# A fused Swin block on one core: values weighed a tile later in one group, channel sums over 128 columns, late products spread over the prologue

## The chip, the cores and the metric

The kernel runs on 1 core of one Trainium2 chip. The metric is the device time of one execution in microseconds; the figure for the kernel before is the median of 3 runs. The engines are TensorE (PE; its weight loads are PEld), VectorE (DVE), ScalarE (ACT), GpSimd (POOL) and SyncE (SP), which here only starts transfers. Each engine works through its own instruction list in order and waits on semaphores for the others.

## The reference

The input x is 16 images of 64 channels and 16 x 16 pixels, fp32. One Swin transformer block, cut to what matters:

```python
xn = roll(layernorm_over_channels(x) * g1 + b1, (-4, -4))
windows = 8x8 windows of xn                      # 64 windows of 64 tokens, 64 channels
q, k, v = split(windows @ in_w.T + in_b)         # 8 heads of 8
attn = softmax(q @ k.T / sqrt(8)) @ v            # per window and head
y = x + roll_back((attn @ out_w.T + out_b) @ proj_w.T + proj_b)
z = layernorm_over_channels(y) * g2 + b2
result = y + (gelu(z @ fc1_w.T + fc1_b) @ fc2_w.T + fc2_b)   # 64 -> 256 -> 64
```

## The kernel before

**Tiles.** The work is cut into 8 tiles (`TILES`) of 256 token columns. A tile holds two images: image w = 0 on the channel partitions 0 to 63, w = 1 on 64 to 127. Everything is fp32; a product on TensorE shows as two records in the trace (two passes). A transposition of 128 x 128 is one record.

**Stages of a tile k.** VectorE takes statistics (`ln1_stats`), GpSimd makes `rstd` and scales; TensorE transposes (`x_transpose`) and projects q, k and v (`project_qkv`), three tiles ahead (`AHEAD`). ScalarE copies q, k, v out of PSUM; SyncE spreads q and k over four head slots by 8 transfers per tile (`mask_heads`, L238). TensorE forms the scores once with queries on partitions, into `ps_s`, for the row maximum on VectorE (`find_max`, L594), and once transposed, into `ps_t` (`scores_both` interleaves the two, L302). The maximum is transposed on VectorE (`transpose_max`) and spread by GpSimd (`spread_max`, L937), and TensorE subtracts it from the transposed scores (`shift_scores`, L359). ScalarE exponentiates (L825) into `probs`. `weigh_values` (L376) multiplies by values and ones, so sums and weighted values come out together in `ps_u`, image by image. On VectorE `normalise` then does four things in a row: transposition of `ps_u` into `sums` (L608), reciprocal (L610), scaling into `attn_tok` (L614), transposition into `attn` (L621). TensorE's `project_out` (L392) applies output and projection weights, folded into one matrix at the start; VectorE's `residual` (L628) adds x. For the second norm ScalarE squares y, TensorE's `y_sum` (L404) sums y and its square over the 64 channels of each image, ScalarE and VectorE make the variance (`ln2_var`, L642), GpSimd the reciprocal root and its widening (`ln2_rstd`, `ln2_widen`), TensorE spreads it (`y_spread`, L419), VectorE scales (`ln2_scale`, L647).

**The order.** It is written out by hand, engine by engine, in functions named `slot(t)`, called for t = 0 to 7 (TensorE has `first_slot` for t = 0). TensorE's slot t holds, in this order, the first scores group of tile t + 1 with the transposed scores of tile t, the shift of (t, 0), `project_qkv(t + 3)`, values of (t - 1, image 1), `y_sum(t - 2)`, the second scores group, the shift of (t, 1), `x_transpose`, `y_spread`, values of (t, image 0), `project_out(t - 1)`. VectorE's slot t holds `find_max(t + 1, 0)`, statistics, the whole of `normalise(t - 1)`, `ln2_var(t - 2)`, `find_max(t + 1, 1)`, `transpose_max(t + 1)`, `residual(t - 1)`, `ln2_scale(t - 3)`.

**Start and end.** Before slot 1, TensorE makes products of the late weights (`late_products`, `fc1_mean`, `bias_of_v`) and runs products of zeros (`warm_up`, L257). After the slots come four steps of 512 columns of the two-layer net, `fc1` (L433), gelu on ScalarE (L853), `fc2` (L449) and VectorE's `finish` (L708), with what is left of the last tiles between them.

**PSUM.** There are 8 banks: `ps_s` 2, `ps_t` 2, `ps_m` 2, `ps_u`, `ps_o`. `ps_u` holds the weighed values of both images of one tile; it is free when `sums` has been transposed. `ps_o` takes `project_out`, `y_sum` and the late products in turn.

## Time and profile before

| | |
|---|---|
| three runs | 97.44, 100.54, 97.42 us; median 97.44 |
| profiled execution, its own time | 97.66 us |
| its span, first to last instruction | 95.8 us |
| mean granted TensorE clock | 0.997 of full |
| busy: PE, DVE, ACT, POOL | 90%, 67%, 50%, 45% of the span |
| transfers | 5.87 MB, 61 GB/s over the span |

The span starts and ends with an instruction; the execution's own time has 1.86 us more around it. A slice or a busy share is an average over stages with different limits, so each stage has to be read by itself: which engine waits last, and for whom.

### The profile page before, as it was taken

Reading aid. Unit: us, or ns where it says so; the run is one execution under the profiler, and the core shown is the slowest. Engines: PE = TensorE matmul, PEld = TensorE weight load, DVE = VectorE, ACT = ScalarE, POOL = GpSimd, SP = SyncE. Lnnn points to the kernel's source line nnn. Section 1 sums busy time; section 2 is a strip of 40 time slices with the busy share of each in tenths; the row PEclk is TensorE's granted clock in tenths of the full one; section 3 lists DMA queues with packets and bytes.
Section 4 is the critical chain, followed back from the end, with each engine's and each line's share of the span. In section 5 each row is a group of like instructions: output and inputs, shape, how many; then the busy total and the mean of one; then the engine's idle time right before and its main releaser. Section 6 shows DMA issues by size and latency. Waiting matters only on the chain.

```text
span 95.8 us, 4276 instructions
## 1 busy us (share of the span) xinstructions
PE 86.4 (90%) x1810; PEld 55.0 (57%) x1810; DVE 63.8 (67%) x183; ACT 48.1 (50%) x78; POOL 43.5 (45%) x56
## 2 busy tenths in 40 slices
PE   5999999999999699999999889989899967799960
PEld 5987756776755557747666567566665224233330
DVE  5966879818899978957959889798342943403070
ACT  0594815735556447556655443335449654073700
POOL 7988734485056436750740834708343063500000
PEclk9999999999999999999999999999999999999998
DMA  2899110111110111111110101000000000020323
GB/s 36 236 383 403 64 42 14 57 48 42 41 46 29 61 42 56 36 47 42 34 61 28 61 28 41 0 7 0 7 0 7 0 0 7 0 109 0 113 107 112
DMA packets 3747, 5.87 MB, mean 61 GB/s; under 512 B 1136, under 2 KB 1904, under 8 KB 3600
## 3 DMA queue, kind: packets, MB, share of 16 engines
q1 hardware_dynamic: 2864, 3.22, 9.9%
q10 hardware_dynamic: 864, 2.38, 6.6%
q8 instruction: 14, 0.23, 1.1%
q14 instruction: 5, 0.04, 0.2%
HBM read 2.64 MB, written 1.05 MB: 39 GB/s over the span
## 4 chain that ended last, share of the span: by engine, by line
PE 32%; issue 24%; POOL 19%; DVE 15%; DMA 3%; SPq 2%; POOLq 1%; ACT 1%; DVEq 0%
POOL max_x L937 7%; POOL rstd L946 7%; PE ps_t L257 6%; DVE row_max L594 6%; POOL rstd_x L953 5%; DMA masked<-qk 3%; PE ps_t L359 3%; PE ps_u L449 3%; PE ps_m L277 3%; DVE sums L608 2%; PE ps_s L302 2%; PE ps_t L433 2%; PE ps_o L449 2%; PE ps_u L376 2%; SPq L238 2%
## 5 line engine op out<-in xcount | busy, mean ns | idle before, releaser
L825 ACT ACTIVATE probs<-ps_t 128x1024 f32<-128x1024 f32 x16 | 16.4, 1024 | 17.4 <-PE ps_t L359 17.4
L594 DVE TENSOR_REDUCE row_max<-ps_s 128x16 f32<-128x1024 f32 x15 | 18.2, 1216 | 5.2 <-PE ps_s L302 5.2
L302 PE MATMUL ps_t<-masked,qk 32*64 32x256 f32 x272 | 18.7, 387 | 0.4 <-ACT probs L825 0.3
L946 POOL TENSOR_TENSOR rstd<-y_var,minus_half 128x4 f32<-128x4 f32 x8 | 8.3, 1034 | 22.0 <-DVE y_var L642 21.8
L302 PE MATMUL ps_s<-masked,qk 32*64 32x256 f32 x240 | 16.5, 386 | 1.7 <-ACT probs L825 0.7
L359 PE MATMUL ps_t<-max_x,minus_sel 128*128 128x512 f32 x32 | 11.7, 446 | 0.8 <-POOL max_x L937 0.8
L302 PEld LDWEIGHTS ps_s<-masked,qk 32*64 32x64 f32 x240 | 8.3, 131 | 4.3 <-issue 2.8
L376 PE MATMUL ps_u<-probs,vz 128*32 128x64 f32 x512 | 10.5, 222 | 0.0
L376 PEld LDWEIGHTS ps_u<-probs,vz 128*32 128x32 f32 x512 | 7.9, 109 | 3.8 <-issue 2.8
L302 PEld LDWEIGHTS ps_t<-masked,qk 32*64 32x64 f32 x272 | 8.7, 131 | 1.5 <-issue 0.4
L257 PE MATMUL ps_t<-zeros 128*128 128x128 f32 x40 | 8.2, 366 | 1.0 <-DVE zeros L737 1.0
L359 PEld LDWEIGHTS ps_t<-max_x,minus_sel 128*128 128x128 f32 x32 | 4.8, 188 | 6.9 <-POOL max_x L937 3.5
L608 DVE STREAM_TRANSPOSE sums<-ps_u 128x512 f32<-128x512 f32 x8 | 5.7, 712 | 4.5 <-PE ps_u L376 4.4
L922 POOL TENSOR_TENSOR rstd<-var,minus_half 128x4 f32<-128x4 f32 x8 | 8.2, 1025 | 0.7
L257 PEld LDWEIGHTS ps_t<-zeros 128*128 128x128 f32 x40 | 7.1, 265 | 1.7 <-DVE zeros L737 1.0
L937 POOL TENSOR_TENSOR max_x<-max_t,early 128x512 fp32r<-128x512 f32 x6 | 6.3, 1050 | 3.0 <-DVE max_t L602 3.0
L953 POOL TENSOR_SCALAR rstd_x<-rstd 128x256 f32<-128x256 f32 x8 | 6.9, 857 | 0.3
L628 DVE SCALAR_TENSOR_TENSOR y_all<-ps_o,b_out,x_ch 128x256 f32<-128x256 f32 x8 | 3.8, 470 | 4.4 <-PE ps_o L392 4.4
L794 ACT ACTIVATE qk<-ps_m,b_qk 128x512 f32<-128x512 f32 x7 | 4.8, 685 | 3.4 <-PE ps_m L289 3.3
L831 ACT ACTIVATE y_sq<-y_all 128x256 f32<-128x256 f32 x8 | 3.3, 416 | 6.2 <-DVE y_all L628 6.2
L919 POOL TENSOR_SCALAR var<-mv 128x4 f32<-128x4 f32 x8 | 1.6, 197 | 10.4 <-DVE mv L587 10.1
L972 POOL MEMSET masked<- 128x2048 f32 x3 | 5.4, 1806 | 2.0 <-DVE row_max L594 2.0
(102 smaller groups left out, 147.8 us busy)
## 6 DMA issues: line engine op xcount, KB each, us to landing
masked<-qk SPq DMA_DIRECT2D x58, 32.0 KB, 1.9
x_ch<-x_ch_d ACTq DMA_DIRECT2D x1, 1024.0 KB, 8.5
out_d<-result SPq DMA_DIRECT2D x3, 256.0 KB, 2.5
x_tok<-x_tok_d ACTq DMA_DIRECT2D x1, 512.0 KB, 6.5
late<-late_d ACTq DMA_DIRECT2D x1, 352.0 KB, 5.1
x_tok<-x_tok_d SPq DMA_DIRECT2D x2, 128.0 KB, 3.2
x_tok<-x_tok_d ACTq DMA_DIRECT2D x1, 256.0 KB, 4.5
out_d<-result SPq DMA_DIRECT2D x2, 128.0 KB, 2.3
```

The costliest lines, as they stand in the source:

```text
L257: nc.tensor.matmul(ps[:, 0, 0:P], zeros[:], zeros[:], start=True, stop=True)
L302: return nc.tensor.matmul(ps[L * u:L * u + L, g, n * TOK:(n + 1) * TOK], qk[r:r + RG, b, w, t], masked[r:r + RG, b, :, w, t], start=(n == ...
L359: ins = nc.tensor.matmul(ps_t[:, g, :], minus_sel[:, 2 * w + g].rearrange("q u j -> q (u j)"), max_x[:, k % 2, :], start=False, stop=True, ...
L376: ins = nc.tensor.matmul(u5[32 * h:32 * h + 32, w, n, :, g, :], vz[:, k % VB, w, n, SLOTS * g + h, :], probs[:, w, c:c + L], start=True, s ...
L594: nc.vector.tensor_reduce(row_max[:, 16 * w:16 * w + 16], score_bank(k, w)[:].rearrange("q g (h j) -> q (g h) j", j=L), axis=AX.X, op=ALU. ...
L608: nc.vector.transpose(sums[:].rearrange("q n r -> q (n r)"), ps_u[:, 0, :]).then_inc(sums_transposed, 1)
L825: nc.scalar.activation(probs[:, w, :], ps_t[:].rearrange("q g c -> q (g c)"), ACT.Exp).then_inc(probs_done, 1)
L922: nc.gpsimd.tensor_tensor(rstd1[:, b, :], var1[:, b, :], minus_half[:], op=ALU.pow).then_inc(x_rstd_done, 1)
L937: nc.gpsimd.tensor_tensor(max_x[:, k % 2, :].rearrange("q (n i) -> q n i", n=16), max_t[:].unsqueeze(1).to_broadcast([P, 16, 32]), spread1 ...
L946: nc.gpsimd.tensor_tensor(rstd2[:].rearrange("q n w -> q (n w)"), y_var[:].rearrange("q n w -> q (n w)"), minus_half[:], op=ALU.pow).then_ ...
L953: nc.gpsimd.tensor_scalar(rstd2_x[:, k % 2].rearrange("q n (w c) -> q n w c", w=2), rstd2[:].unsqueeze(3).to_broadcast([P, BLK, 2, C]), 1. ...
L972: nc.gpsimd.memset(masked[:, b].rearrange("q h w t -> q (h w t)"), 0.0).then_inc(masked_zeroed[b], 1)
```

## The change

It has five parts.

1. `weigh_values` of both images of tile t - 1 now stand together in slot t, followed by `project_out(t - 2)` (before: `project_out(t - 1)` at the slot's end). `probs` has four buffers in place of two, so exponentiate waits for the values of two tiles back.
2. `y_sum` takes 128 columns as stationary operand: 4 products of 128 x 2 in place of 16 of 32 x 2. It stands at the end of the slot, after `y_spread`.
3. VectorE's `normalise` is split in four. Transposition of the sums and reciprocal stay ahead of `find_max(t + 1, 1)`, with `residual(t - 2)` between the two; scaling and transposition of the attention come behind `transpose_max`. `ln2_var` and `ln2_scale` move to the front of the next slot. ScalarE's squaring of y and GpSimd's `ln2_rstd` and `ln2_widen` move accordingly.
4. The late products are split: those of the output weights between the projections of q, k and of v of tile 0, the bias products between `x_transpose(2)` and `project_qkv(2)`, `fc1_mean` and `bias_of_v` into slot 1. Nine of twelve `warm_up` products behind the first projection go.
5. The end has another order, since the last tiles are one stage further back; the second-to-last spread uses `ps_o`.

The core of the diff:

```diff
-        probs = sb("probs", [P, 2, 1024])
+        probs = sb("probs", [P, 4, 1024])
...
-                        for j in range(4):
-                            c = n * P + 32 * j
-                            src = y_sq[:, c:c + 32] if s else y_all[:, k * TOK + c:k * TOK + c + 32]
-                            ins = nc.tensor.matmul(ps_o[32 * j:32 * j + 32, 0, 4 * n + 2 * s:4 * n + 2 * s + 2], src, ones2,
-                                                   start=True, stop=True, tile_position=(0, 32 * j))
+                        c = n * P
+                        src = y_sq[:, c:c + P] if s else y_all[:, k * TOK + c:k * TOK + c + P]
+                        ins = nc.tensor.matmul(ps_o[:, 0, 4 * n + 2 * s:4 * n + 2 * s + 2], src, ones2,
+                                               start=True, stop=True)
...
                 x_transpose(2)
-                warm_up(2, ps_u)
+                late_products_bias()
                 project_qkv(2)
-                late_products()
-                warm_up(2, ps_u)
                 scores_both(1, 0, 0, 1)
                 shift_scores(0, 1)
                 x_transpose(3)
-                weigh_values(0, 0)
                 scores(1, 1)
                 project_qkv(3)
-                fc1_mean()
-                bias_of_v()
...
                 if t == 1:
+                    fc1_mean()
+                    bias_of_v()
+                    weigh_values(0, 0)
                     weigh_values(0, 1)
                 if tile_ok(t + AHEAD):
                     project_qkv(t + AHEAD)
                 if t >= 2:
+                    weigh_values(t - 1, 0)
                     weigh_values(t - 1, 1)
-                    y_sum(t - 2)
+                    project_out(t - 2)
...
                 if t >= AHEAD:
                     y_spread(t - AHEAD)
-                weigh_values(t, 0)
...
-                project_out(t - 1)
...
+                if t >= 2:
+                    y_sum(t - 2)
...
             project_qk(0)
-            warm_up(4)
+            late_products_out()
+            warm_up(2)
             project_v(0)
-            warm_up(2)
             scores(0, 0)
...
-            warm_up(2, ps_u)
+            warm_up(1, ps_u)
...
+            fc1(0, 0)
+            weigh_values(TILES - 1, 0)
+            weigh_values(TILES - 1, 1)
+            project_out(TILES - 2)
             fc1(0, 1)
+            y_spread(TILES - 3)
             y_sum(TILES - 2)
             fc1(1, 0)
             project_out(TILES - 1)
             fc1(1, 1)
-            y_spread(TILES - 2)
             y_sum(TILES - 1)
             fc2(0)
+            y_spread(TILES - 2)
+            fc1(2, 0)
             y_spread(TILES - 1)
-            fc1(2, 0)
...
-                if k >= 1:
-                    act.wait_ge(values_weighed, 2 * (k - 1) + w + 1)
+                if k >= 2:
+                    act.wait_ge(values_weighed, 2 * (k - 2) + w + 1)
```

**TensorE's order in the middle of slot 2**, behind `project_qkv(5)` and ahead of the second scores group: what went has a minus, what came a plus. A row names the line, the tile written and the tiles read, and the output's shape; L376 are values, L404 the channel sums, L392 `project_out`, L302 the scores.

```order
-L376 MATMUL ps_u<-probs,vz 32x2x32 x16
-L404 MATMUL ps_o<-early,y_all 32x2 x4
-L404 MATMUL ps_o<-early,y_sq 32x2 x4
-L404 MATMUL ps_o<-early,y_all 32x2 x4
-L404 MATMUL ps_o<-early,y_sq 32x2 x4
+L376 MATMUL ps_u<-probs,vz 32x2x32 x32
+L392 MATMUL ps_o<-attn,w_out 32x2x64 x8
 L302 MATMUL ps_s<-masked,qk 64x256 x4
 L302 MATMUL ps_t<-masked,qk 64x256 x4
```

The values of both images now stand together (x32), `project_out` follows them, and the sums of y are gone from here.

**TensorE at the end of slot 2**, behind the second shift (L359) and `x_transpose` (L266):

```order
 L359 MATMUL ps_t<-max_x,minus_sel 128x512 x2
 L266 MATMUL ps_m<-ident_sb,xhat 128x128 x2
-L376 MATMUL ps_u<-probs,vz 32x2x32 x16
-L392 MATMUL ps_o<-attn,w_out 32x2x64 x8
+L403 MATMUL ps_o<-early,y_all 128x2
+L403 MATMUL ps_o<-early,y_sq 128x2
+L403 MATMUL ps_o<-early,y_all 128x2
+L403 MATMUL ps_o<-early,y_sq 128x2
```

The values of the current tile and `project_out` have gone; the sums of y, now 4 products (L403), end the slot.

**VectorE in a steady slot (slot 4), before**, from one first maximum (L594 as first row) to the end of the slot:

```order
L594 TENSOR_REDUCE row_max<-ps_s 128x16
L608 STREAM_TRANSPOSE sums<-ps_u 128x512
L610 RECIPROCAL recip<-sums 128x32
L614 TENSOR_TENSOR attn_tok<-sums,recip 128x256
L621 STREAM_TRANSPOSE attn<-attn_tok 128x256
L642 SCALAR_TENSOR_TENSOR y_var<-ps_o,y_msq 128x4
L594 TENSOR_REDUCE row_max<-ps_s 128x16
L602 STREAM_TRANSPOSE max_t<-row_max 128x32
L628 SCALAR_TENSOR_TENSOR y_all<-ps_o,b_out,x_ch 128x256
L647 TENSOR_TENSOR z_all<-y_all,ps_m 128x256
```

And now the rows that correspond (L608 sums, L612 reciprocal, L618 `attn_tok`, L627 `attn`, L634 residual, L648 and L653 variance and scaling of the second norm, which belong to the next slot):

```order
L594 TENSOR_REDUCE row_max<-ps_s 128x16
L608 STREAM_TRANSPOSE sums<-ps_u 128x512
L634 SCALAR_TENSOR_TENSOR y_all<-ps_o,b_out,x_ch 128x256
L612 RECIPROCAL recip<-sums 128x32
L594 TENSOR_REDUCE row_max<-ps_s 128x16
L602 STREAM_TRANSPOSE max_t<-row_max 128x32
L618 TENSOR_TENSOR attn_tok<-sums,recip 128x256
L627 STREAM_TRANSPOSE attn<-attn_tok 128x256
L648 SCALAR_TENSOR_TENSOR y_var<-ps_o,y_msq 128x4
L653 TENSOR_TENSOR z_all<-y_all,ps_m 128x256
```

Between the sums and the second maximum there are now residual and reciprocal; scaling and transposition of the attention and the variance stand behind the maximum.

## Rows read from the trace of the kernel before

**Rows 1.** The page, part 1: busy us, share of the span, instructions.
```profile
PE 86.4 (90%) x1810; PEld 55.0 (57%) x1810; DVE 63.8 (67%) x183; ACT 48.1 (50%) x78; POOL 43.5 (45%) x56
```

**Rows 2.** Timeline, TensorE, slot 4: start us, duration us, operation [idle before <-releaser].
```profile
48.24 0.73 PE L359 MATMUL ps_t<-max_x,minus_sel 128*128 128x512 f32 x2 [0.20 <-POOL max_x L937]
48.90 0.66 PE L277 MATMUL ps_m<-xn,w_qkv 64*64 64x256 f32 x8
...
49.73 0.65 PE L376 MATMUL ps_u<-probs,vz 128*32 128x64 f32 x32
50.20 0.22 PE L404 MATMUL ps_o<-early,y_all 128*32 128x2 f32 x8
...
50.58 0.45 PE L302 MATMUL ps_s<-masked,qk 32*64 32x256 f32 x4
...
51.63 0.73 PE L359 MATMUL ps_t<-max_x,minus_sel 128*128 128x512 f32 x2
...
52.51 0.65 PE L376 MATMUL ps_u<-probs,vz 128*32 128x64 f32 x32
52.98 0.62 PE L392 MATMUL ps_o<-attn,w_out 128*32 128x128 f32 x16
...
55.10 0.73 PE L359 MATMUL ps_t<-max_x,minus_sel 128*128 128x512 f32 x2 [0.20 <-POOL max_x L937]
```

**Rows 3.** Timelines of VectorE and then GpSimd, same slot.
```profile
50.45 0.72 DVE L608 STREAM_TRANSPOSE sums<-ps_u 128x512 f32<-128x512 f32 x1 [1.16 <-PE ps_u L376]
...
51.59 0.42 DVE L614 TENSOR_TENSOR attn_tok<-sums,recip 128x256 f32<-128x256 f32 x1
...
52.46 1.21 DVE L594 TENSOR_REDUCE row_max<-ps_s 128x16 f32<-128x1024 f32 x1
...
53.84 0.44 DVE L628 SCALAR_TENSOR_TENSOR y_all<-ps_o,b_out,x_ch 128x256 f32<-128x256 f32 x1
...
53.99 1.05 POOL L937 TENSOR_TENSOR max_x<-max_t,early 128x512 fp32r<-128x512 f32 x1 [0.34 <-DVE max_t L602]
```

**Rows 4.** Timeline of TensorE, slots 0 to 2.
```profile
17.06 0.61 PE L257 MATMUL ps_u<-zeros 128*128 128x128 f32 x4
...
19.09 0.60 PE L462 MATMUL ps_o<-early,late 64*128 64x1 f32 x4
19.56 0.36 PE L464 MATMUL ps_o<-early,late 64*128 64x1 f32 x2
...
20.49 0.45 PE L302 MATMUL ps_s<-masked,qk 32*64 32x256 f32 x4
...
24.85 0.70 PE L469 MATMUL ps_o<-w_fc_s,mean_w 64*128 64x256 f32 x2
...
34.54 0.73 PE L359 MATMUL ps_t<-max_x,minus_sel 128*128 128x512 f32 x2 [0.20 <-POOL max_x L937]
```

**Rows 5.** Timelines of VectorE and then ScalarE, slot 0.
```profile
21.65 1.23 DVE L594 TENSOR_REDUCE row_max<-ps_s 128x16 f32<-128x1024 f32 x1 [2.12 <-PE ps_s L302]
...
2.13 0.45 ACTq L874 DMA_DIRECT2D late<-late_d  x1
...
17.54 1.02 ACT L825 ACTIVATE probs<-ps_t 128x1024 f32<-128x1024 f32 x1
```

**Rows 6.** Transfers: SyncE's timeline, the chain of waits, the page's part 6.
```profile
19.37 2.90 SPq L238 DMA_DIRECT2D masked<-qk  x4
...
11.94 3.27 DMA masked<-qk
...
masked<-qk SPq DMA_DIRECT2D x58, 32.0 KB, 1.9
...
late<-late_d ACTq DMA_DIRECT2D x1, 352.0 KB, 5.1
```

**Rows 7.** End: timeline of TensorE, then that of VectorE.
```profile
67.23 0.73 PE L359 MATMUL ps_t<-max_x,minus_sel 128*128 128x512 f32 x2
...
77.46 0.65 PE L392 MATMUL ps_o<-attn,w_out 128*32 128x128 f32 x16 [0.90 <-DVE y_var L642]
...
92.77 0.48 DVE L708 SCALAR_TENSOR_TENSOR result<-ps_m,early,y_all 128x256 f32<-128x256 f32 x1 [0.28 <-PE ps_m L449]
```

More of the change, by code:

```diff
@@ L376, in weigh_values @@
                             ins = nc.tensor.matmul(u5[32 * h:32 * h + 32, w, n, :, g, :],
-                                                   vz[:, k % VB, w, n, SLOTS * g + h, :], probs[:, w, c:c + L],
+                                                   vz[:, k % VB, w, n, SLOTS * g + h, :], probs[:, (2 * k + w) % 4, c:c + L],
                                                    start=True, stop=True, tile_position=(0, 32 * h))
@@ L414, in y_spread @@
                 elif k == TILES - 2:
-                    pe.wait_ge(sums_transposed, TILES)
+                    pe.wait_ge(y_var_done, TILES)
                 elif k == TILES - 1:
-                    pe.wait_ge(y_var_done, TILES)
+                    pe.wait_ge(z_done, TILES - 1)
                 for n in range(BLK):
@@ L440, in fc2 @@
                 if s == 0:
-                    pe.wait_ge(z_done, TILES - 1)
+                    pe.wait_ge(sums_transposed, TILES)
                 if s == 1:
@@ L460, in late_products, with late_products_bias @@
                                      start=True, stop=True)
+            def late_products_bias():
                 for m in range(M2):
@@ L520, in slot @@
                     y_spread(t - AHEAD)
-                weigh_values(t, 0)
-                if not more:
-                    fc1(0, 0)
-                    weigh_values(t, 1)
-                project_out(t - 1)
-                if not more:
-                    y_spread(TILES - 3)
+                if t >= 2:
+                    y_sum(t - 2)
             pe.wait_ge(zeros_set, 1)
@@ L608, in normalise, with invert_sums, scale_attn @@
                 nc.vector.transpose(sums[:].rearrange("q n r -> q (n r)"), ps_u[:, 0, :]).then_inc(sums_transposed, 1)
+            def invert_sums(k):
                 dve.wait_ge(sums_transposed, k + 1)
                 nc.vector.reciprocal(recip[:], sums[:, :, 2 * D:2 * D + 2]).then_inc(recip_done, 1)
+            def scale_attn(k):
                 dve.wait_ge(recip_done, k + 1)
@@ L617, in normalise, with transpose_attn @@
                                         op=ALU.mult).then_inc(attn_scaled, 1)
+            def transpose_attn(k):
                 dve.wait_ge(attn_scaled, k + 1)
@@ L712, in slot @@
             def slot(t):
+                if tile_ok(t - AHEAD):
+                    ln2_var(t - AHEAD)
+                if tile_ok(t - AHEAD - 1):
+                    ln2_scale(t - AHEAD - 1)
                 if tile_ok(t + 1):
@@ L716, in slot @@
                     late_weights()
-                elif tile_ok(t + AHEAD + 2):
+                if t == 1:
+                    late_bias()
+                if t >= 1 and tile_ok(t + AHEAD + 2):
                     ln1_stats(t + AHEAD + 2)
                 if tile_ok(t - 1):
-                    normalise(t - 1)
+                    transpose_sums(t - 1)
                 if tile_ok(t - 2):
-                    ln2_var(t - 2)
+                    residual(t - 2)
+                if tile_ok(t - 1):
+                    invert_sums(t - 1)
                 if tile_ok(t + 1):
@@ L728, in slot @@
                     ln1_stats(AHEAD + 2)
-                    late_bias()
                     dve.wait_ge(vz_zeroed, 2)
@@ L732, in slot @@
                 if tile_ok(t - 1):
-                    residual(t - 1)
-                if tile_ok(t - AHEAD):
-                    ln2_scale(t - AHEAD)
+                    scale_attn(t - 1)
+                    transpose_attn(t - 1)
             nc.vector.memset(zeros[:], 0.0).then_inc(zeros_set, 1)
@@ L769, in _ @@
                 slot(t)
+            ln2_scale(TILES - 4)
+            ln2_var(TILES - 3)
+            transpose_sums(TILES - 1)
+            invert_sums(TILES - 1)
+            residual(TILES - 2)
+            scale_attn(TILES - 1)
             ln2_scale(TILES - 3)
-            normalise(TILES - 1)
+            transpose_attn(TILES - 1)
             ln2_var(TILES - 2)
             residual(TILES - 1)
+            ln2_var(TILES - 1)
             ln2_scale(TILES - 2)
-            ln2_var(TILES - 1)
             finish(0)
@@ L822, in exponentiate @@
                 act.wait_ge(scores_shifted, 2 * k + w + 1)
-                if k >= 1:
-                    act.wait_ge(values_weighed, 2 * (k - 1) + w + 1)
-                nc.scalar.activation(probs[:, w, :], ps_t[:].rearrange("q g c -> q (g c)"), ACT.Exp).then_inc(probs_done, 1)
+                if k >= 2:
+                    act.wait_ge(values_weighed, 2 * (k - 2) + w + 1)
+                nc.scalar.activation(probs[:, (2 * k + w) % 4, :], ps_t[:].rearrange("q g c -> q (g c)"), ACT.Exp).then_inc(probs_done, 1)
             def square_y(k):
@@ L861, in slot @@
                 if tile_ok(t - 2):
-                    square_mean(t - 2)
+                    square_y(t - 2)
                 exponentiate(t, 1)
@@ L865, in slot @@
                     copy_xn(t + AHEAD + 1)
-                if tile_ok(t - 1) and tile_ok(t + 1):
-                    square_y(t - 1)
+                if tile_ok(t - 2):
+                    square_mean(t - 2)
             act.dma_start(early[:], early_d).then_inc(early_loaded, 16)
@@ L960, in slot @@
             def slot(t):
+                if tile_ok(t - AHEAD):
+                    ln2_rstd(t - AHEAD)
+                    ln2_widen(t - AHEAD)
                 if tile_ok(t + AHEAD + 2):
@@ L963, in slot @@
                     ln1_scale(t + AHEAD + 2)
-                if tile_ok(t - 2):
-                    ln2_rstd(t - 2)
                 if t >= 1 and tile_ok(t + 1):
                     spread_max(t + 1)
-                if tile_ok(t - 2):
-                    ln2_widen(t - 2)
             def zero_masked(b):
@@ L993, in _ @@
                 slot(t)
-            for k in (TILES - 2, TILES - 1):
+            for k in range(TILES - 3, TILES):
                 ln2_rstd(k)
```

6 lines of the change are left out of this document (3 added, 3 removed).

## The prediction

> **What bounds the kernel now.** The page's busy row puts TensorE at 90% [rows 1], which invites the reading "bound by TensorE". The timeline of one steady slot, read next, says otherwise. From the shift of tile 4 at 48.24 to that of tile 5 at 55.10, TensorE's work, taken as differences of neighbouring starts, is 0.66 shift, 0.83 projections, 0.47 values, 0.38 `y_sum`, 1.05 scores, 0.88 shift and `y_spread`, 0.47 values, then 0.62 `project_out` by its own row and again 1.05 scores: 6.4 us of a period of 6.86. The rest it waits, 0.20 of it visibly for GpSimd ahead of the next shift [rows 2].
>
> What fills 6.86 is a ring. With T = 48.24: VectorE's transposition of the sums begins at T + 2.21, after shift, projections and values of one image. Then 1.14 for sums (0.72) and reciprocal, 0.87 for `attn_tok`, attention transposition and `y_var`, 1.53 from the maximum's start (1.21 long) to GpSimd's, 1.11 until TensorE shifts again [rows 2, 3]. The sum is 6.86. Without projections (slots 5 and 6) it is 0.83 shorter, 6.03; shift to shift I read 55.10 to 67.23, two slots of 6.07 [rows 2, 7]. So **the ring VectorE, GpSimd, TensorE decides, with TensorE only 0.4 us behind it**. An edit must shorten the ring without adding more than that to TensorE.
>
> **The ring after the change.** Out of it: `scale_attn`, `transpose_attn` and `ln2_var`, -0.87, now behind the maximum. Into it: the second image's values, +0.47, and the residual, which now stands between sums and reciprocal, 0.44 [rows 3], of which some 0.03 runs under its neighbour, so +0.41. The residual also waits for `project_out(t-2)`, begun on TensorE at T + 2.43 and done at T + 3.1; the sums end only at T + 3.4, so it is ready. Ring: 6.86 - 0.87 + 0.88 = **6.87, unchanged**; 6.04 without projections. The scores of the next tile must be there too: they start at T + 3.03, and a maximum starts 1.16 after its scores (20.49 to 21.65, [rows 4, 5]), at T + 4.19, just before the reciprocal is done (T + 4.2). What leaves the ring runs in VectorE's idle time behind the maximum, done at T - 0.3 of the next slot; `project_out` wants it at T + 2.4. On GpSimd `ln2_rstd` no longer stands ahead of the maximum's spreading; it had been over before that began (it stood idle ahead of 53.99, [rows 3]), so that is worth nothing. Likewise the four `probs` buffers: exponentiate waits for nothing new, and TensorE's wait for probabilities in slots 5 and 6 moves to the slot's end.
>
> **`y_sum` with 128 columns.** Before: 16 products of 32 columns, 0.38 us [rows 2]. After: 4 products, each in two passes as all fp32 products here, so 8 records with a 128-column weight load. No such row with 2 moving columns over 128 partitions exists. The nearest above: products of 128 columns with one moving column, over 64 partitions: four records from 19.09 to 19.56, 0.117 each [rows 4], so 8 x 0.117 = **0.94 us**. Below: the same 1,024 columns are loaded as before, so 0.38. Upper end: if record after record waited for the one ahead, 0.60 - 3 x 0.117 = 0.25 each, 2.0 us. I take 0.94, the row that has the load's width: 32-column loads can sit side by side in the array, a full-width load has no neighbour. That adds 0.56 to each of 8 tiles.
>
> The Trainium skill ("TensorE: Matmul & The Clock Gate", LDWEIGHTS) lets a weight load take its column count over 1.2 in ns: 107 ns for 128 columns, near the 0.117 measured; for 32 columns 27 ns, so 32 loads would have taken 0.85 us and the edit would cost nothing. The row of before, 0.38, contradicts that second half. By that rule the time would be that of rival 1.
>
> **TensorE's own slot after.** 6.4 + 0.56 = 6.96, plus 0.22 in slots 2 and 3, where `x_transpose` stands too, less 0.1 since values now lead straight to values and `project_out` (one change of tile shape fewer), less 0.22 in slot 2, which has no `y_spread`. So slot 2: `y_sum` ends T + 5.8, probabilities (exponentiate from T + 4.8, 1.02 long) release the scores at T + 5.85, period 6.9. Slot 3: 7.05, bound by TensorE. Slot 4: 6.9. Slots 5 and 6, by the probabilities of the second half (T + 5.05) and the scores: 6.1 each. Sum 33.05 against 34.54 to 67.23, 32.69: **+0.35**.
>
> **Start.** Before, scores of tile 1 start at 20.49 behind late products and warm-ups, though the probabilities they wait for are ready at 17.54 + 1.02 = 18.56 [rows 4, 5]. Now: bias products, six records at 0.117 and a change of shape, 0.75 from 17.06, projections 0.83, scores at 18.65: 1.85 earlier. The other late products stand before 10.1 in place of warm-ups, under the wait for the first qk copy; their data left at 2.13 and takes 5.1, so landed by 7.3 [rows 5, 6]. What the removed warm-ups did ahead of 15.2 costs nothing, because the transfer of the first masked tile, started at 11.94, ends at 15.21 in any case [rows 6]. Then: maximum 19.81 to 21.04; second scores 21.08, maximum 22.24 to 23.48, `spread_max_dve` by 24.4. The scores of tile 2 start when that maximum is done, 23.5; their masks, four issues from 19.37 of some 0.6 each, the last at 21.2 and 1.9 in flight, landed at 23.1 [rows 6]. Shift of tile 1: 23.5 + 1.05 + 0.22 = 24.8. Slot 1 now carries `fc1_mean` and the bias products (0.84, the former with 0.70 in rows 4) and two groups of values: 24.8 + 0.6 + 0.84 + 1.0 + 0.83 = 28.1, scores; VectorE has sums (from 28.4, behind `late_bias` and the statistics) and reciprocal done at 29.5, then maximum 1.24, 0.29, GpSimd 1.1: shift of tile 2 at **32.1, 2.4 earlier** than 34.54. No attention work stands in between any more; half of the gain is that.
>
> **End.** From the shift of tile 7 (67.23) to the last result's addition (92.77): 25.5, in which TensorE's waits by its timeline add up to 2.2, 0.90 the largest [rows 7]. Now three `y_sum` lie here (+1.7), one more `project_out` (+0.62), one more group of values (+0.47): +2.8. The waits go, since `y_var` of tile 6 no longer is last and the final spreading has `fc2(0)` and `fc1(2,0)` over it; about 0.3 for squaring tile 6 behind the first gelu stays. Some 0.5 comes back where equal shapes now follow each other (values on values twice, `project_out` on both, sums on spreads; 0.1 each, as above). 25.5 - 2.2 + 2.8 + 0.3 - 0.5 = 25.9, **+0.4**: the reordering nearly pays for its own additions.
>
> **Sum.** -2.4 + 0.35 + 0.4 = -1.7 (rounded from -1.65). Span 95.8 to 94.1; the profiled execution, 97.66, becomes 96.0 and stood 0.22 over the median of 97.44. Against the median: **95.7 us**. A measurement of this kernel tells 2% from no change, so the bounds are 95.5 and 99.4.
>
> **Rivals.**
> 1. *Narrow and full loads cost alike by columns* (`y_sum` stays 0.38). What speaks for it: the number of columns is the same, and the 0.117 row was over 64 partitions and between other shapes. What speaks against it: the only loads of that width before products this short were spaced 0.117. Slot 3 -0.15, slots 5 and 6 -0.1, end -1.0 (three times 0.56, less what the waits take back): 94.4. Chance 0.16.
> 2. *The start isn't given back*: scores of tile 2 depend on masks whose issue is unchanged, since the copy of qk stays behind exponentiate. The last transfer of tile 0 took 3.3 instead of 1.9 [rows 6]: then 24.5 instead of 23.5, 96.7. If the statistics or `late_bias` on VectorE hold up the sums of tile 0 as well, another 1: 97.7. Chance 0.22.
> 3. *Slower: loads and products of `y_sum` don't overlap.* Place: end of each slot, ahead of the scores, where nothing else runs on TensorE. Price: 2.0 us instead of 0.94, 8 times: +8.5, 104.2. It decides from 1.40 us per `y_sum` on, (99.4 - 95.7) / 8 above my 0.94; before that, from 1.16, the gain is gone. The spacing of 0.117 speaks against it. A smaller form is a TensorE that is slower at each change of tile shape. Chance 0.10.
> 4. Forecast, 94.9 to 96.5: 0.52.
>
> Faster: 0.45 of the forecast's 0.52 and rival 1, 0.40. Within 2%: the rest of it and nearly all of rival 2, 0.48. Slower: rival 3 and the upper edge of rival 2, 0.12. The range 93.8 to 97.9 takes in the forecast and rivals 1 and 2.
>
> **What would show it.** `y_sum` from its first start to the next scores: 0.94 (rival 1: 0.4; rival 3: from 1.4). Shift of tile 1 at 24.8, tile 2 at 32.1, tile 7 at 65.2; late if rival 2 holds. From there on 29.0 to the end, 28.6 before. In a steady slot sums, residual, reciprocal and maximum in one row on VectorE with no gap. Wrong I would be above all in the start, whose recurrence has most steps, or in the end, where losses and waits of 2 to 3 us cancel.

## The result: 99.62 us against 97.46

The changed kernel takes 99.62 us (median of 4 runs), the kernel before 97.46 us in the same session: ratio 1.0215, 95% interval 1.0166 to 1.0264. It is slower, clear of the noise; the interval leaves open whether by more than 2%. Ratios, here and below, compare the fast executions of both kernels, while medians take in all. The forecast was 95.7, the range 93.8 to 97.9. The profiled execution took 99.92 us with a span of 98.1; the forecast for it was 96.0 and 94.1.

The page of the changed kernel: busy us, the granted clock in 40 slices (tenths), and TensorE's instruction fetches (transfers, MB, share):

```profile
PE 89.0 (91%) x1600; PEld 57.6 (59%) x1600; DVE 62.7 (64%) x183; ACT 48.1 (49%) x78; POOL 44.2 (45%) x56
PEclk9999999999999999999999998599999999999999
q8 instruction: 13, 0.21, 0.9%
```

TensorE's share is 91%, where it was 90% [rows 1]. The clock row has a dent at about 61 us. Now TensorE's timeline, the first piece from slots 3 and 4:

```profile
39.30 0.73 PE L359 MATMUL ps_t<-max_x,minus_sel 128*128 128x512 f32 x2
...
40.78 1.09 PE L376 MATMUL ps_u<-probs,vz 128*32 128x64 f32 x61
42.04 0.30 PE L376 MATMUL ps_u<-probs,vz 128*32 128x64 f32 x3 [0.17 <-issue]
42.16 0.65 PE L392 MATMUL ps_o<-attn,w_out 128*32 128x128 f32 x16
...
44.79 0.28 PE L403 MATMUL ps_o<-early,y_all 128*128 128x2 f32 x2
...
45.72 0.45 PE L302 MATMUL ps_s<-masked,qk 32*64 32x256 f32 x4
...
46.77 0.73 PE L359 MATMUL ps_t<-max_x,minus_sel 128*128 128x512 f32 x2
```

`y_sum` takes 0.93 us, from 44.79 to 45.72. The values of both images take 1.38 (40.78 to 42.16); in slot 5, below, the same 64 records take 0.92. The 0.46 us more is one gap near 42, and its releaser reads "issue": TensorE waited for nothing that the profile shows. (The row gives 0.17 idle, since the ends of products are modelled; from start to start 0.46 is lost.) The second piece, slot 5 and the start of slot 6:

```profile
53.77 0.73 PE L359 MATMUL ps_t<-max_x,minus_sel 128*128 128x512 f32 x2
54.43 1.10 PE L376 MATMUL ps_u<-probs,vz 128*32 128x64 f32 x64
55.35 0.62 PE L392 MATMUL ps_o<-attn,w_out 128*32 128x128 f32 x16
55.90 0.45 PE L302 MATMUL ps_s<-masked,qk 32*64 32x256 f32 x4
...
57.39 0.43 PE L302 MATMUL ps_t<-masked,qk 32*64 32x256 f32 x2 [0.82 <-issue]
...
58.40 0.73 PE L359 MATMUL ps_t<-max_x,minus_sel 128*128 128x512 f32 x2
...
60.34 0.59 PE L302 MATMUL ps_s<-masked,qk 32*64 32x256 f32 x4 [0.20 <-ACT probs L843]
60.63 0.72 PE L302 MATMUL ps_s<-masked,qk 32*64 32x256 f32 x4
...
62.20 1.22 PE L359 MATMUL ps_t<-max_x,minus_sel 128*128 128x512 f32 x2
```

One group of scores takes 2.50 us (55.90 to 58.40), where the kernel before has 1.05 [rows 2]. It stops halfway, again with the releaser "issue". From 60.3 on the same instructions take nearly twice as long (the shift 1.22 for 0.73): the granted clock is at the lower of its two levels until 63.9. VectorE in slot 4:

```profile
49.43 0.72 DVE L608 STREAM_TRANSPOSE sums<-ps_u 128x512 f32<-128x512 f32 x1 [1.34 <-PE ps_u L376]
50.07 0.44 DVE L634 SCALAR_TENSOR_TENSOR y_all<-ps_o,b_out,x_ch 128x256 f32<-128x256 f32 x1
50.43 0.34 DVE L612 RECIPROCAL recip<-sums 128x32 f32<-128x32 f32 x1
50.89 1.23 DVE L594 TENSOR_REDUCE row_max<-ps_s 128x16 f32<-128x1024 f32 x1
52.15 0.21 DVE L602 STREAM_TRANSPOSE max_t<-row_max 128x32 f32<-128x32 f32 x1
```

Sums, residual, reciprocal and maximum stand in a row, as forecast, with at most 0.12 us between two of them. GpSimd's spreading of the maximum ends 6.81 us behind the slot's first shift (46.77 to 53.58), where a ring of 6.87 was forecast. The ring isn't what was lost.

### The profile page after: what moved, and what is told of

Read it like the earlier page. It is cut to its first block, busy times and chain, and to the rows that moved or that the text cites. A ratio compares the mean times of both kernels' runs of the same rounds, so it can differ in the third digit from the quotient of the medians.

```text
span 98.1 us, 3854 instructions
## 1 busy us (share of the span) xinstructions
PE 89.0 (91%) x1600; PEld 57.6 (59%) x1600; DVE 62.7 (64%) x183; ACT 48.1 (49%) x78; POOL 44.2 (45%) x56
## 2 busy tenths in 40 slices
DMA packets 3746, 5.85 MB, mean 60 GB/s; under 512 B 1136, under 2 KB 1904, under 8 KB 3600
## 3 DMA queue, kind: packets, MB, share of 16 engines
HBM read 2.64 MB, written 1.05 MB: 38 GB/s over the span
## 4 chain that ended last, share of the span: by engine, by line
PE 75%; ACT 7%; DMA 6%; SPq 4%; issue 3%; DVE 2%
PE ps_s L302 12%; PE ps_t L359 10%; PE ps_u L376 9%; PE ps_t L257 6%; PE ps_t L302 6%; DMA masked<-qk 6%; ACT probs L843 5%; PE ps_u L448 5%; PE ps_m L277 4%; PE ps_o L403 4%; SPq L238 4%; PE ps_o L392 3%; PE ps_s L432 3%; PE ps_m L432 2%; PE ps_t L432 2%
## 5 line engine op out<-in xcount | busy, mean ns | idle before, releaser
L594 DVE TENSOR_REDUCE row_max<-ps_s 128x16 f32<-128x1024 f32 x15 | 18.4, 1225 | 6.9 <-PE ps_s L302 6.6
L302 PE MATMUL ps_t<-masked,qk 32*64 32x256 f32 x272 | 20.0, 401 | 1.6 <-issue 0.8
L302 PE MATMUL ps_s<-masked,qk 32*64 32x256 f32 x240 | 17.4, 402 | 2.8 <-ACT probs L843 1.5
L955 POOL TENSOR_TENSOR max_x<-max_t,early 128x512 fp32r<-128x512 f32 x6 | 6.8, 1132 | 19.8 <-DVE max_t L602 19.8
L359 PE MATMUL ps_t<-max_x,minus_sel 128*128 128x512 f32 x32 | 12.2, 463 | 0.0
L302 PEld LDWEIGHTS ps_s<-masked,qk 32*64 32x64 f32 x240 | 8.4, 134 | 5.6 <-issue 2.9
L608 DVE STREAM_TRANSPOSE sums<-ps_u 128x512 f32<-128x512 f32 x8 | 5.7, 713 | 9.0 <-PE ps_u L376 9.0
L302 PEld LDWEIGHTS ps_t<-masked,qk 32*64 32x64 f32 x272 | 9.3, 134 | 3.2 <-issue 1.9
L376 PE MATMUL ps_u<-probs,vz 128*32 128x64 f32 x512 | 9.3, 224 | 0.2 <-issue 0.2
L376 PEld LDWEIGHTS ps_u<-probs,vz 128*32 128x32 f32 x512 | 7.9, 112 | 2.7 <-issue 2.5
L359 PEld LDWEIGHTS ps_t<-max_x,minus_sel 128*128 128x128 f32 x32 | 5.0, 195 | 6.1 <-issue 4.2
L257 PE MATMUL ps_t<-zeros 128*128 128x128 f32 x32 | 6.8, 374 | 1.0 <-DVE zeros L749 1.0
L257 PEld LDWEIGHTS ps_t<-zeros 128*128 128x128 f32 x32 | 5.9, 272 | 1.3 <-DVE zeros L749 1.0
L834 ACT ACTIVATE vz<-ps_m 64x256 f32<-64x256 f32 x16 | 5.9, 371 | 0.2
L403 PE MATMUL ps_o<-early,y_sq 128*128 128x2 f32 x32 | 5.8, 251 | 0.0
```

The lines of the kernel that those rows point to most:

```text
L257: nc.tensor.matmul(ps[:, 0, 0:P], zeros[:], zeros[:], start=True, stop=True)
L302: return nc.tensor.matmul(ps[L * u:L * u + L, g, n * TOK:(n + 1) * TOK], qk[r:r + RG, b, w, t], masked[r:r + RG, b, :, w, t], start=(n == ...
L359: ins = nc.tensor.matmul(ps_t[:, g, :], minus_sel[:, 2 * w + g].rearrange("q u j -> q (u j)"), max_x[:, k % 2, :], start=False, stop=True, ...
L376: ins = nc.tensor.matmul(u5[32 * h:32 * h + 32, w, n, :, g, :], vz[:, k % VB, w, n, SLOTS * g + h, :], probs[:, (2 * k + w) % 4, c:c + L], ...
L403: ins = nc.tensor.matmul(ps_o[:, 0, 4 * n + 2 * s:4 * n + 2 * s + 2], src, ones2, start=True, stop=True)
L594: nc.vector.tensor_reduce(row_max[:, 16 * w:16 * w + 16], score_bank(k, w)[:].rearrange("q g (h j) -> q (g h) j", j=L), axis=AX.X, op=ALU. ...
```

## The experiments

**Theory C** (the code supply): TensorE's instructions come in blocks of 256, one transfer of queue q8 each. Where the engine uses a block up before the next has come, it stands still with nothing to wait for. A boundary is the place in TensorE's list where one block ends and the next begins. The first expectations say Theory S for its general form (standstills that belong to the code), and Theory Y for the rival that `y_sum` and TensorE's own work make every slot longer. **Rivals**: the changed order or VectorE's ring costs the time, or `y_sum` does. The instruction transfers and how many records had run by then are read from the trace's records; an fp32 product has four instructions (two weight loads, two multiplications).

### 1. The changed kernel again

> The changed kernel once more, nothing altered. Theory S (stalls): in its first profile TensorE stood still in the middle of the transposed scores of tile 5 (56.2 to 57.4) and of the values of tile 2 (0.47 us) with nothing to wait for, and ran at half clock from 60.3 to 63.8; these cost 3.5 us of 98.1. If they belong to the code, they stand at the same instructions again and the time is 99.3 within 0.4. Theory Y (the forecast's slot is too short everywhere, y_sum above all): the shift of tile 7 is again about 4 us late with no standstill to be found, spread over slots 2 to 6.

Measured: 100.77 us, ratio 1.0284 [1.0238, 1.033]. The profile has the same stop at the same instruction, and the fall of the clock behind it:

```profile
58.06 0.43 PE L302 MATMUL ps_t<-masked,qk 32*64 32x256 f32 x2 [1.09 <-issue]
```

The stop in slot 5 belongs to the kernel, not to one execution. The small one of slot 3 is smaller here: the slot takes 7.21 us for 7.47, and no row has the releaser "issue".

### 2. Without the wide channel sums

```diff
-  src = ...[c:c + P]; matmul(ps_o[:, 0, ...], src, ones2)          # 4 products
+  for j in range(4): matmul(ps_o[32 * j:32 * j + 32, 0, ...], ...)  # 16, as before the change
```

> The changed kernel with y_sum in its old form, 16 products of 32 columns. y_sum was 0.93 us before the next scores in the changed kernel and 0.38 before. Theory Y: the slots are bound by TensorE, so 0.5 us comes back in 3 to 6 slots and 1.5 us at the end: 96.5 to 97.3. Theory S: the number of TensorE instructions goes back up by 192 products and the standstill moves or goes; 0.2 per slot at most comes back, since scores then wait for the probabilities: 97.5 to 99 if the standstill stays, 95.5 if it goes.

Measured: 98.37 us median, from 95.67 to 100.85. In the fastest, profiled run (95.67, full clock) slots 5 and 6 take 6.17 and 6.41, but slots 2 to 4 stay at 6.99: the scores wait up to 0.6 there for ScalarE's probabilities. What follows the shift of tile 7 takes 27.5 us, 1.6 less, three times 0.55. This profile has no stop at all, though the values of both images stand together in it: the group alone doesn't make a stop.

### 3. The wide sums alone, in the kernel before

> The kernel before with nothing but y_sum over 128 columns, in its old place ahead of the second scores. There it stands in front of the scores, and the second maximum waits for the scores: they had 1.0 us of slack over the maximum, so 0.55 more per y_sum is hidden in slots 3 and 4, and partly in 5 and 6 where the probabilities bind. Theory Y: +0.3 to +2.5 (97.7 to 100). Theory S: fewer instructions could bring the standstill into this kernel as well, seen as an idle stretch of TensorE over 0.4 us without a releaser.

Measured: 100.58 us median, 99.76 in the profiled execution, ratio 1.0196 [1.0157, 1.0234]. In the profile the clock is full, and there is no stop at a boundary. Slots 2 to 6 are longer by 1.3 in all, the rest is at the end. So the wide sums alone cost about as much as the whole change.

### 4. The changed kernel with its instructions moved by 112 places

```diff
-            warm_up(8)
+            warm_up(4)
+            for i in range(32):       # short products of zeros, 32 columns, 2 moving
+                j = i % 4
+                nc.tensor.matmul(ps_t[32 * j:32 * j + 32, 0, 0:2], zeros[:, 32 * j:32 * j + 32], zeros[:, 0:2], ...)
```

> The changed kernel with 4 of the first 8 warm-up products replaced by 32 narrow ones, so that all later TensorE instructions lie 112 places further on in its code; the work behind is the same and the warm-up ends before it is waited for. Theory S, if the standstill comes from the supply of instructions: it moves to another place in the work, and the time changes by up to 1.5 us either way. If the standstill belongs to the work itself: same place, same time. Theory Y: same time as the changed kernel, 99.3.

```profile
36.00 0.27 PE L376 MATMUL ps_u<-probs,vz 128*32 128x64 f32 x2 [0.41 <-issue]
...
50.98 0.43 PE L392 MATMUL ps_o<-attn,w_out 128*32 128x128 f32 x8 [0.43 <-issue]
```

Measured: profiled 98.67 us. The stops have moved to slots 2 and 4 (7.73 and 7.63 us long), and slots 3 and 5 no longer have any; slots 5 and 6 take 6.16 and 6.27. What the program does in slots 3 and 5 is unchanged: only the place in the list of instructions is another. The unprofiled runs took 100.22 to 106.19 us; experiment 9 bears on that.

### 5. Values ungrouped, all else as changed

```diff
                 if t >= 2:
-                    weigh_values(t - 1, 0)
                     weigh_values(t - 1, 1)
...
+                weigh_values(t, 0)        # end of the slot, behind y_sum
```

> The changed kernel with the values of image 0 back at the end of the slot of their own tile; y_sum over 128 columns, the later project_out and the new start stay. Theory C (code supply: TensorE's instructions come in 16 KB blocks, and in each of six profiles it stood still only where it reached the next block less than fetch time + 1.4 us after the fetch had begun): the densest stretch, 64 value records, 16 of project_out and 32 of scores in 2.5 us, is thinned to 32 + 16 + 32, so the standstills of 1.2 us and the clock fall behind them go: 96 to 97.5. Rival Y (y_sum and TensorE's own work set the slots): no more than 0.3 comes back, 99 to 100.

Measured: 97.81 us, ratio 0.9982 [0.9947, 1.0017]; profiled 97.00. No stop anywhere; slots 2 to 6 take 6.85, 7.08, 6.85, 6.29, 6.27. Ungrouped, the change gets 2 to 3 us back. Like experiment 2, this is one alignment of the blocks; that ungrouped values have no stop in any isn't shown, and experiment 11 has a small one.

### 6. One idle stretch put into the kernel before

```diff
+                if t == 5:
+                    pe.wait_ge(attn_done, 5)     # ahead of the second scores
```

> The kernel before with one more wait on TensorE: in slot 5, ahead of the second scores, for the attention of tile 4, which by the profile of before comes 1.5 us later. Theory K (the standstill takes the clock down): TensorE idles 1.8 us at 57, and the granted clock falls to half some 2.5 us later, as it did behind both standstills of over 1.2 us; cost 1.5 + about 1.5 = 3.0, 100.4. Rival: the clock falls for another reason, TensorE's load over a longer time: it stays full and the cost is 1.5, 98.9, or 1.2 if the ring takes some.

```profile
PEclk9999999999999999999999995799999999999999
58.76 0.45 PE L302 MATMUL ps_s<-masked,qk 32*64 32x256 f32 x4 [1.90 <-DVE attn L623]
```

Measured: 99.85 us, ratio 1.015 [1.0115, 1.0186]. In the profile (100.82) the clock is at half from 59.6 to 63.0. The four runs fall into 99.06 and 99.13 on one side, 100.58 and 100.82 on the other. An idle stretch of 1.9 us, made by a semaphore, is followed by a fall like that of the changed kernel. The two pairs of runs differ by about 1.6, the price of the fall; the mean granted clock is 1.0 in the first pair and 0.983 in the second.

### 7. Only the new start, in the kernel before

> The kernel before with nothing but the spread late products and the nine fewer warm-ups (fc1_mean, bias_of_v and the values stay where they were). The forecast gave half of the 2.4 us gained by the shift of tile 2 to this. Theory: scores of tile 1 start 1.85 earlier, of that 1.2 to 1.8 is left at the shift of tile 2, and nothing behind it changes: 95.7 to 96.3. Theory C adds that the code is moved by 20 to 40 instructions, which can bring in a standstill of up to 1.2 us. Rival: the start's gain is lost at the masks' transfers, 97.0 to 97.4.

Measured: 95.78 us, ratio 0.9806 [0.9782, 0.9829]. Its profile is of a longer execution (97.78), in which TensorE idles 1.23 us for the first masked tile and the clock then falls:

```profile
15.66 1.09 PE L302 MATMUL ps_t<-masked,qk 32*64 32x256 f32 x16 [1.23 <-DMA masked<-qk]
...
18.32 1.13 PE L277 MATMUL ps_m<-xn,w_qkv 64*64 64x256 f32 x8
```

The start alone is worth 1.9 us.

### 8. Ungrouped values and the old sums together

> As e5, and y_sum in its old form of 16 products. From the profiles y_sum costs nothing in a slot (scores wait for the probabilities either way, 0.2 or 0.6 us) and 3 x 0.55 at the end: 1.6 less than e5, 94.5 to 96. Theory C: the 64 more records per y_sum make other stretches denser, a standstill of 0.2 to 0.5 may come in. Rival Y: more than 2 less than e5.

Measured: 94.88 us, ratio 0.9692 [0.9648, 0.9736], though the profiled run has the clock fall at 18.4 us. It beats both kernels. The sign named for Rival Y (`y_sum` and TensorE's own work set the slots) came in all the same: it is 2.9 us below experiment 5, not 1.6. Behind the shift of tile 7 1.7 less is spent, as expected, but slots 2 to 6 are shorter too, 6.55, 6.56, 6.67, 5.97 and 6.18, 1.4 in sum. So with the values ungrouped `y_sum` does cost time in the slots. And against experiment 2, where the slots stay at 6.99 without any stop, the group costs 0.3 to 0.4 in each of slots 2 to 4, where the second image's values, 0.47, stand ahead of the second scores.

### 9. Moved by 48 places

> The changed kernel, in which four of the first eight products of zeros are replaced by 16 short ones (32 columns in, 2 out); nothing behind them is altered, but TensorE's instructions all stand 48 places later in its list. Theory C (TensorE is held at every 256th instruction if the fetch of the next block, begun some 60 instructions behind the boundary ahead, hasn't ended): by the changed kernel's trace the boundaries now fall where the rest of the block is used up in 1.9 us at about 35.5 (second scores of tile 3) and 1.9 us at about 50.2 (second scores of slot 4), and in 2.7 us near 55.5; so standstills of 0.3 to 1.5 us with nothing to wait for at the first two, perhaps the third, and none at 42.0 or 57.4. Profiled time 98 to 100.5. Rival (the standstills belong to the place in the program, or to VectorE's ring): idle at 42.0 in the values of slot 3 and at 57.4 in the second scores of slot 5 again, whatever stands ahead.

```profile
63.90 0.62 PE L392 MATMUL ps_o<-attn,w_out 128*32 128x128 f32 x10 [0.27 <-issue]
...
19.35 1.98 PE L302 MATMUL ps_t<-masked,qk 32*64 32x256 f32 x16
```

Measured: profiled 105.48 us, 98.56 in the best of four runs. The second row is why: to about 30 us everything on TensorE takes nearly twice its time (1.98 for 1.09), so all times lie some 8 us later in the middle of the kernel (7.7 from slot 4 on). The engine works at the pace of its lower level for that long, and the page's clock row doesn't show it; the trace's own records of the clock begin with a rise to the full level at 29.48 us, where those of the changed kernel begin with one at 5.90. In experiments 4 and 10, which also lack full-size products of zeros at the start, the rise is at 10.82 and 10.16. That these products decide it isn't shown: experiments 5 and 8 have all eight, and each has one execution of about 105 us too (105.59, 104.77). Read with 7.7 taken off, the stops are at 50.4 (slot 4, 0.24) and 56.2 (slot 5, 0.66), two of the three places named, and none is at 42.0 or 57.4. The first place (35.5) only came near: the block had landed 1.9 us before its first instruction ran, those of the two stops 1.4.

### 10. Moved by 208 places

> The changed kernel, in which all of the first eight products of zeros are replaced by 60 short ones; TensorE's instructions behind them stand 208 places later. Theory C: by the changed kernel's trace only the boundary near 42.8 (first scores of slot 3) comes 2.3 us after the fetch could begin, all others 3.7 us or more. So at most one small standstill there (under 0.4 us), slots 4 to 6 near 7.0, 6.2 and 6.2, no later fall of the clock, profiled time 95.8 to 96.8, the prediction's own figure. Rival (the changed order itself costs the 3 to 4 us): standstills or slots as long as in the changed kernel (7.5 in slot 3, 8.4 in slot 5), time 99.5 or more.

```profile
60.75 1.10 PE L376 MATMUL ps_u<-probs,vz 128*32 128x64 f32 x64
61.66 0.62 PE L392 MATMUL ps_o<-attn,w_out 128*32 128x128 f32 x16
62.22 0.65 PE L302 MATMUL ps_s<-masked,qk 32*64 32x256 f32 x4
63.87 0.43 PE L302 MATMUL ps_s<-masked,qk 32*64 32x256 f32 x2 [1.01 <-issue]
```

Measured: profiled 99.31 us; a miss in the total. Slots 2 to 5 are clean, 7.00, 6.98, 7.00 and 6.17, which is within 0.1 each of the forecast's 6.9, 7.05, 6.9 and 6.1. But slot 6 has a stop that I had ruled out (7.78 long), behind the same dense stretch: the block's transfer began at 61.58, 3.6 us behind the boundary before it, where I had reckoned with about one. (The next block came late as well, for a stop of 0.16 idle at 69.99.) The boundaries can be foretold, the start of a fetch could not. The rival that the stops belong to places of the program is refuted by four alignments with four sets of places (experiments 1, 4, 9 and 10); that a lucky alignment saves the changed kernel was my own guess and failed.

### 11. The best version, its first idle stretch filled

```diff
-            warm_up(1, ps_u)
+            warm_up(4, ps_u)
```

> The version with values ungrouped, old channel sums and the new start, with three more products of zeros ahead of TensorE's wait for the first masked tile (idle there 1.18 us before, now about 0.5). If that idle stretch is what takes the clock down at 18.4 us for 3.4 us, the clock stays full, tile 1's shift starts 1.2 to 1.8 us earlier and the profiled time is 93.3 to 94.0. If the fall has another cause, it is there again and the time stays at 95.

```profile
15.25 1.09 PE L302 MATMUL ps_t<-masked,qk 32*64 32x256 f32 x16 [0.15 <-DMA masked<-qk]
...
45.32 0.63 PE L376 MATMUL ps_u<-probs,vz 128*32 128x64 f32 x26 [0.25 <-issue]
```

Measured: 93.91 us, ratio 0.958 [0.9543, 0.9618]: the best of all, and 5.7% under the changed kernel. The clock stays full, though in this very run TensorE idles 1.38 us for the masks of tile 2:

```profile
24.46 0.45 PE L302 MATMUL ps_s<-masked,qk 32*64 32x256 f32 x4 [1.38 <-DMA masked<-qk]
```

Tile 1's shift comes 1.04 us earlier, a little less than expected; the wait for those masks takes part of the gain. A small stop is left (0.25 idle).

### 12. The supply by itself

The kernel before, and behind its last product:

```diff
+            pe.wait_ge(result_done, 3)
+            for i in range(512):
+                j = i % 4
+                nc.tensor.matmul(ps_o[32 * j:32 * j + 32, 0, 0:64], zeros[:, 32 * j:32 * j + 32], zeros[:, 0:64],
+                                 start=True, stop=True, tile_position=(0, 32 * j))
```

> The kernel before, with 512 products of zeros of the values' form (32 columns loaded, 64 moving, 2,048 instructions of TensorE) put behind everything else, where TensorE waits for nobody; its end grows by their time, which is what is measured. In the kernel before such products take 0.47 us per 16 (64 instructions), so 512 of them 15 us if TensorE is never short of instructions (rival: the standstills come from the ring or the semaphores of the kernel). Theory C: after every 256 instructions, which take 1.9 us, the next block is there only 2.9 to 3.8 us after the previous one (fetch 0.9 to 1.5 us, 1.45 us to its first instruction, and the delay to the start of the fetch), so eight times 2.9 to 3.8 us, 23 to 30 us, with standstills of 1 to 1.9 us at distances of 256 instructions, each with one transfer of the instruction queue.

TensorE's timeline, and q8 in the window from 93 us on:

```profile
92.61 2.55 PE L574 MATMUL ps_o<-zeros 128*32 128x64 f32 x166
96.17 1.99 PE L574 MATMUL ps_o<-zeros 128*32 128x64 f32 x128 [1.02 <-issue]
99.62 1.99 PE L574 MATMUL ps_o<-zeros 128*32 128x64 f32 x128 [1.46 <-issue]
103.35 1.99 PE L574 MATMUL ps_o<-zeros 128*32 128x64 f32 x128 [1.73 <-issue]
107.08 1.99 PE L574 MATMUL ps_o<-zeros 128*32 128x64 f32 x128 [1.73 <-issue]
...
117.99 1.53 PE L574 MATMUL ps_o<-zeros 128*32 128x64 f32 x90 [1.46 <-issue]
...
q8 instruction: 7, 0.11, 1.9%
```

This is theory C in the open: 128 multiplications with their 128 weight loads, 256 instructions, then a stop of up to 1.73 us, again and again, seven stops with seven transfers. At its longest a block takes 3.73 us, of which the engine works 1.99; the products take 27 us where 15 would do, and the execution grows by 24.0 (121.56 for 97.59). By the records a block's transfer starts 0.7 to 1.1 us behind the first instruction of the block before and takes 1.0 to 1.4, and 1.2 to 1.5 later its first instruction runs.

## Why the prediction was wrong

**Right.** `y_sum`: 0.94 forecast, 0.93 measured. The row with the load's width decided against rival 1. Of the rule of the Trainium skill that the prediction gives ("TensorE: Matmul & The Clock Gate", LDWEIGHTS) the figure for 128 columns fits: eight times 107 ns is 0.86, an estimate, for 0.93 measured. The one for 32 columns doesn't, as the 0.38 of before had said. The start: shifts of tiles 1 and 2 forecast at 24.8 and 32.1, measured at 24.93 and 32.31; alone it gave 1.9 us (experiment 7). The end: 29.0 from the shift of tile 7 forecast, 29.04 measured. The ring: unchanged, and in clean slots 7.0 and 6.17 where 6.9 to 7.05 and 6.1 were forecast; 0.28 over five slots. In slot 4 it is the probabilities that set the scores free, as forecast, at T + 5.95 for 5.85; GpSimd's spreading of the maximum now takes 1.13 for 1.05 [rows 3], but it is done before the scores are.

**Wrong.** The step that failed is "TensorE's own slot after", 6.4 + 0.56: it added up TensorE's work by the rows and took for granted that the engine is handed instructions as fast as it runs them. The shift of tile 7 was forecast at 65.2 and came at 69.06 in the profiled execution, 3.9 us late:

| | us |
|---|---|
| shift of tile 2, 32.31 for 32.1 | 0.2 |
| five slots at their clean length, 7.0 x 3 + 6.17 x 2 for 33.05 | 0.3 |
| stop in slot 3: 7.47 for 7.00 | 0.5 |
| stop in slot 5: scores 2.50 for 1.05 | 1.45 |
| half clock, 60.3 to 63.9: slots 5 and 6 took 8.43 + 6.86 for 2 x 6.17, less the 1.45 | 1.5 |

The sum, 3.95, is the 3.9 within the rounding. So in this execution the expected gain of 1.7 was there but for 0.5, and 3.4 of stops and clock came on top.

The last row is of executions with a fall of the clock. Two of the changed kernel's four runs had the full clock (1.0) and still took 99.25 and 99.33, 1.8 us more than before; no trace of them was kept, so where their time went is open.

The mechanism, by the records of slot 5: the boundary before is passed at 52.72. The next block's transfer starts at 54.73, 2.0 us later, takes 1.10, and 1.56 behind its landing the first instruction of the block runs, at 57.39. The work between the two boundaries takes about 3.6, so the engine stands from about 56.3, and the group of scores ends 1.45 late. Two things come together. The first is the pace: the change puts 128 instructions of values, 32 of `project_out` and 64 of scores in a row, 224 in 2.5 us (54.43 to 56.95 had it not stopped), that is 256 in 2.9 us, while in experiment 12 a new block comes every 3.73. The second is the late start of the transfer: had it begun 1.1 behind the boundary, as in experiment 12, the block would have been there some 0.9 us sooner and most of the stop gone (an estimate). In the kernel before, 64 instructions of values, 64 of the old sums and 64 of scores stood there, denser (192 in 1.9 us) but shorter, and behind them came the long products of the shift; from slot 1 on no transfer of it starts more than 1.5 behind its boundary, and there is one near miss, at 57.6 in slot 5, that costs about 0.1. That the length of the stretch makes the difference is my reading; no run varied the length alone. Nothing in the rows I chose showed this.

The count of instructions tells such a stop from other waits. Number TensorE's records (weight loads, multiplications and its semaphore records) from the first: divided by 256, the number of the first instruction behind a stop leaves the same remainder each time, 192 or 193. In the changed kernel they are 1473 and 2240, in experiment 4 1216 and 1985, in experiment 9 2241, in experiment 10 2753 and 3008, in experiment 11 1729, and in experiment 12 all seven, from 4033 on. The releaser alone wouldn't do. The kernel before has it too:

```profile
33.21 0.45 PE L302 MATMUL ps_s<-masked,qk 32*64 32x256 f32 x4 [0.51 <-issue]
```

That is number 997, remainder 229, and VectorE's maximum, whose bank these scores need, had ended at 33.12: by these two an ordinary wait. In experiment 7 the same wait of 0.51 happens to fall on remainder 193, but its block had landed 4.3 us before; so count and transfer belong together.

So: that the supply of 256-instruction blocks makes the stops is shown by experiment 12 and by the count, and that they go with the alignment by 4, 9 and 10. That the group has a part is shown by experiment 5 in one alignment only; experiment 2 has the group without a stop and experiment 11 a small stop without the group.

The Trainium skill ("Runtime: NRT & Kernel Launch", Instruction fetch mechanics) says that the queue is refilled in blocks of 256 instructions, and that the fetch is hidden, since the engine dispatches more slowly than the blocks come. The first half agrees with experiment 12. The second doesn't, for TensorE with short products: seven of seven blocks came late.

The clock: in the changed kernel, its repetition and experiment 6 a stop of 1.2 to 1.9 us is followed some 1 to 3 us later by a stretch at the lower level (60.5 to 63.9 in the first). At the start, idling 1.23 and 1.18 us (experiments 7 and 8) was followed by such a fall. But idling 1.12 us at the same place in experiment 2, 1.36 at 24.4 us in experiment 1 and 1.38 at 24.5 us in experiment 11 was not, nor was the stop in slot 6 of experiment 10, which cost 1.6, nor were the stops of 1.7 in experiment 12, where 128 multiplications take 1.99 us each time. So the 1.5 us belong to the stop only in the sense that no profile has a fall without a stop or an idle stretch ahead of it; what decides stays open. That experiment 11's extra products of zeros kept the clock up is likewise not shown.

**The rivals.** None was the case. Rival 1 (0.38) and rival 3 (2.0) are refuted by 0.93, rival 2 by the shift at 32.31. The slower side had 0.12, all of it on `y_sum` and the start. Experiment 3 shows what the other parts had to pay for: the wide sums alone cost the kernel before 2%.

**Open.** Why some fetches (the transfers of blocks) start 1.9 to 3.8 us behind the boundary before (39.49 and 54.73 in the changed kernel, 61.58 in experiment 10), where most start within 1.5, isn't in the traces. The stops of 0.4 us and more in the kernels all followed such late ones, but not each late one made a stop: that of 61.19 in the changed kernel, 3.8 behind, had a slow stretch before it and did no harm.

## What to carry to other kernels

Count instructions beside microseconds: here TensorE had 224 instructions in 2.5 us with no wait between. Where you see the like, look for "issue" in its waits, check whether the distance between such stops is 256 instructions or a multiple, and try a stretch of long products between short ones rather than collecting them (a suggestion; no run tested it by itself). A reordering that removes idle time from an engine may also remove the time in which its code arrives. Take a change apart before judging it: here one part (the start) was good, one (the wide sums) bad, one (the group) bad because it lengthens the slots and, in the changed kernel's alignment, by a resource that no busy share shows. With both undone and three more products of zeros at the start the same idea gives 93.91 us.

## What the runs showed of the hardware

- TensorE's code arrives in blocks of 256 instructions; back to back, up to 3.73 us per block, of which products of four instructions and 0.03 us each fill 53% (experiment 12).
- The stop's place moves with the number of instructions ahead of it, even if these are only products of zeros at the start.
- In one execution of a kernel with full-size products of zeros replaced by short ones at the start, later groups took 1.98 us for 1.09 until about 30 us, while the page's clock row stood at 9 (experiment 9). Of the eight timed runs of experiments 9 and 10 six took 105 us or more; of the eighteen of experiments 5 and 8, with all eight products, two took about 105.
- The old channel sums, 32 loads of 32 columns in 0.38 us [rows 2], are cheaper than 8 of 128 columns in 0.93, for the same columns.
